# Cross-attention, first batch: the root in two halves, rows scaled on two engines, and new orders around the first scores

## What is computed

```python
Sim = (e @ w1)[:, :, None] + (ctx @ w2)[:, None, :] + einsum('bid,bjd->bij', e * w3, ctx) + b_sim   # e = layernorm(x)
A = softmax(Sim, axis=2)
hq_hat = einsum('bij,bjd->bid', A, ctx)
Batt = softmax(max(Sim, axis=2), axis=1)
hc_bar = einsum('bi,bid->bd', Batt, e)                       # one row for each batch
hcq = concat([e, hq_hat, e * hq_hat, e * hc_bar]) @ W_qv + b_qv
x = x + tanh(g_xattn) * hcq
x = x + tanh(g_ffn) * expert_attention(layernorm(x))         # 8 heads, 5 experts; not touched by the change
```

## Time and profile before

| | |
|---|---|
| time, median of 3 runs | 1182.5 us (1181.83 to 1182.51) |
| the profiled execution's own time | 1181.56 us |
| its span, first to last instruction | 1179.8 us |
| PE busy | 1165.9 us (99%) |
| DVE, ACT, POOL busy | 834.1, 647.7, 657.9 us (71%, 55%, 56%) |
| granted clock of TensorE, mean | 1.000 |

### The profile page before, as it was taken

One profiled execution on the slowest core, in us unless ns is written; L12 is line 12 of the kernel. 1 busy time (PEld: TensorE's weight loads), 2 busy tenths in 40 slices (PEclk: granted clock), 3 DMA queues, 4 the chain that ended last, 5 costly groups with the idle time before them and its releaser, 6 DMA issues.

```text
span 1179.8 us, 19684 instructions
## 1 busy us (share of the span) xinstructions
PE 1165.9 (99%) x6377; PEld 909.4 (77%) x6377; DVE 834.1 (71%) x1518; ACT 647.7 (55%) x1444; POOL 657.9 (56%) x476
## 2 busy tenths in 40 slices
PE   7999999999999999999999999999999999999998
PEld 6888888888888888877767777677677777777765
DVE  7888787878787857465775766666666765765868
ACT  6534343434343434477656566557657666665654
POOL 2625242424242425459298397497497396495594
PEclk9999999999999999999999999999999999999999
DMA  5341413132323224401002002002002011020020
GB/s 201 139 134 53 127 65 113 68 110 70 107 78 99 80 63 157 149 8 37 1 5 103 0 18 89 0 27 80 0 36 71 0 58 49 0 71 0 0 72 36
DMA packets 40749, 75.92 MB, mean 64 GB/s; under 512 B 3728, under 2 KB 4240, under 8 KB 40720
## 3 DMA queue, kind: packets, MB, share of 16 engines
q1 hardware_dynamic: 40720, 75.55, 19.2%
HBM read 58.76 MB, written 16.78 MB: 64 GB/s over the span
## 4 chain that ended last, share of the span: by engine, by line
PE 94%; DVE 4%; issue 1%; ACT 1%; DMA 0%; DVEq 0%; SPq 0%
PE ps_f L945 22%; PE ps_r L2018 13%; PE ps_o L2088 9%; PE ps_s L2075 8%; PE ps_s L2067 8%; PE ps_h L945 7%; PE ps_s L945 7%; PE ps_r L2027 6%; PE ps_r L2051 4%; PE ps_r L2033 1%; PE ps_r L2009 1%; PE ps_r L2041 1%; DVE z_tmp L1705 1%; DVE z L1705 1%; PE ps_t L998 1%
## 5 line engine op out<-in xcount | busy, mean ns | idle before, releaser
L1691 DVE TENSOR_REDUCE nmax<-ps_s 128x1 f32<-128x512 f32 x256 | 158.8, 683 | 112.9 <-PE ps_s L2067 111.9
L1522 ACT ACTIVATE tmp<-ps_s,nmax 128x512 f32<-128x512 f32 x256 | 172.7, 687 | 94.1 <-DVE nmax L1691 94.1
L1465 POOL TENSOR_TENSOR z<-z,z_tmp 128x1280 f32<-128x1280 f32 x35 | 102.9, 2941 | 166.2 <-DVE z_tmp L1705 163.9
L1447 POOL TENSOR_TENSOR spare<-xv,pick 128x512 f32<-128x512 f32 x160 | 169.4, 1059 | 35.6 <-DVE pick L1800 22.7
L1453 POOL TENSOR_TENSOR spare<-spare 128x512 f32<-128x512 f32 x128 | 181.7, 1419 | 10.0
L1531 ACT ACTIVATE pt<-ps_s 128x512 f32<-128x512 f32 x256 | 132.1, 612 | 10.5 <-PE ps_s L2075 10.5
L2075 PE MATMUL ps_s<-ident,tmp 128*128 128x128 f32 x1024 | 122.3, 273 | 0.0
L2075 PEld LDWEIGHTS ps_s<-ident,tmp 128*128 128x128 f32 x1024 | 115.4, 140 | 8.6 <-issue 1.6
L2088 PE MATMUL ps_o<-pt,spare 128*64 128x512 f32 x496 | 113.3, 598 | 0.0
L253 POOL TENSOR_TENSOR e_t<-e_t 128x512 fp32r<-128x512 f32 x28 | 35.4, 1299 | 136.4 <-ACT e_t L493 136.4
L2067 PE MATMUL ps_s<-k,q 64*128 64x512 f32 x768 | 107.0, 409 | 0.1
(11 more groups left out here) (234 smaller groups left out, 2119.4 us busy)
## 6 DMA issues: line engine op xcount, KB each, us to landing
stage<-in_x SPq DMA_DIRECT2D x32, 256.0 KB, 3.1
x_sb<-in_x SPq DMA_DIRECT2D x8, 1024.0 KB, 5.2
x_dram<-x_sb SPq DMA_DIRECT2D x32, 256.0 KB, 2.9
stage<-x_dram SPq DMA_DIRECT2D x8, 1024.0 KB, 5.5
x_sb<-x_dram SPq DMA_DIRECT2D x8, 1024.0 KB, 5.4
out_dram<-x_sb SPq DMA_DIRECT2D x32, 256.0 KB, 2.0
stage<-in_ctx_t SPq DMA_DIRECT2D x28, 256.0 KB, 3.0
stage<-in_ctx SPq DMA_DIRECT2D x28, 256.0 KB, 2.6
```

Of the source, the lines that this page charges most:

```text
L1447: pool.tensor_tensor(v_tmp[:] if e else acc, xv[:, :, e, :].unsqueeze(2).broadcast_to(shape), pick[:, 0, e, :, 2 * p:2 * p + 2].unsqueeze( ...
L1465: pool.tensor_tensor(zv, zv, z_tmp[:, h % 2], ALU.add).then_inc(z_pool, 1)
L1522: act.activation(probs[:, n % BANKS, :], ps_s[:, n % BANKS, :], ACT.Exp, bias=nmax[:, n:n + 1], accum_out=den[:, h, t:t + 1]).then_inc(p_e ...
L1691: dve.tensor_reduce(nmax[:, n:n + 1], ps_s[:, n % BANKS, :], AX_X, ALU.max, negate=True).then_inc(nmax_ready, 1)
```

## The change

It touches the first batch of cross-attention alone; the loop over the other batches keeps its instructions and their order, and only some waits of POOL ahead of it differ. The number of matmuls is the same but for the filling transpositions, of which 45 (18+12+3+3+3+6) become 37 (18+8+4+2+3+2).

- SP loads x tiles 0 and 1, then two blocks of transposed context, then `w_cols`, then the other x tiles and blocks.
- The inverse root is taken for tiles 0 and 1 alone, all 17 steps; for tiles 2 and 3 the steps are strewn between other work of DVE. DVE has 17 more tiny instructions.
- `first_scaled` of tiles 0, 1 and 2 moves to ACT (four ACTIVATE Identity of 128 columns with a scale and a bias column); tile 3 stays on DVE, and its last instruction waits for the tile before.
- PE starts to fill after one tile's statistics and not three; the turning of tiles 2 and 3 moves into the scores of tile 1, ahead of its last three matmuls; `turn_a(1)` and `turn_a(2)` stand together behind `scores(3)`.
- On ACT, casts of context, of weights and of the turned probabilities have new places; `probs_hi` of tiles 1, 2 and 3 stand together at the end.
- On DVE, the root of the second batch runs as a whole behind `row_totals`; `first_row_lo`, `row_weights_max` and the second batch's `normalise_x` have new places in `attended`: tiles 2 and 3 are normalised behind `row_shares`.
- POOL's first `add_bias` waits for `wec_lo` and no longer for `wec_ready`, and the next two for the row dots of the second batch.

```diff
-                elif not first:
+                else:
...
+            def load_first_x(tiles):
+                for t in tiles:
+                    sp.dma_start(stage[:, t, :], of(x_dram, 0)[:, t, :]).then_inc(slot_loaded[t], 16)
+
+            def load_first_ctx_t(tiles):
+                for k in tiles:
...
-            load_x(0, True)
+            load_first_x((0, 1))
+            load_first_ctx_t((0, 1))
             sp.dma_start(w_cols[:], w_sim_cols).then_inc(cols_loaded, 16)
-            load_first_ctx_t()
+            load_first_x((2, 3))
+            load_first_ctx_t((2, 3))
...
-            pool.wait_ge(wec_ready, ND)
+            pool.wait_ge(wec_lo, ND)
             add_bias(0, 0)
+            pool.wait_ge(ew1_ready, 2 * NT)
             add_bias(0, 1)
             add_bias(0, 2)
...
+            def first_scaled(t):
+                act.wait_ge(et_ps, t + 1)
+                if t == 0:
+                    act.wait_ge(cols_loaded, 16)
+                for k in range(ND):
+                    last = act.activation(tmp[:, k, t * P:(t + 1) * P], first_turned[t][:, k, :], ACT.Identity,
+                                          bias=w2_col[:, k:k + 1], scale=w3_col[:, k:k + 1])
+                last.then_inc(es_ready, 1)
...
+            def first_root(half, parts):
+
+                tiles = slice(2 * half, 2 * half + 2)
+                for part in parts:
+                    if part == 0:
+                        dve.wait_ge(stats_done, 2 * half + 2)
+                    mean_rstd(dve, part, stats[:, tiles, :], D, mean[:, tiles], work[:, :, tiles], rstd[:, tiles],
+                              newton if half else first_newton, 0)
+
+            def first_normalise(t):
+                dve.wait_ge(newton if t >= 2 else first_newton, ROOT_STEPS)
...
+                    if k == ND - 1:
+
+                        dve.wait_ge(es_ready, t)
                     last = dve.tensor_scalar(tmp[:, k, t * P:(t + 1) * P], first_turned[t][:, k, :], w3_col[:, k:k + 1],
...
-                normalise_x(0, 0)
-                normalise_x(0, 1)
+                row_stats(0, 0, True)
+                row_stats(0, 1, True)
+                first_root(0, range(ROOT_PARTS))
+                first_normalise(0)
+                first_normalise(1)
+                row_stats(0, 2, True)
+                row_stats(0, 3, True)
                 ctx_t_lo(0, 0, True)
-                first_scaled(0)
+                first_root(1, range(5))
+                first_scaled_lo(0)
                 ctx_t_lo(0, 1, True)
-                normalise_x(0, 2)
-                first_scaled_lo(0)
+                first_root(1, (5, 6))
                 ctx_t_lo(0, 2, True)
+                first_root(1, (7,))
                 ctx_t_lo(0, 3, True)
-                first_scaled(1)
-                normalise_x(0, 3)
+                first_root(1, (8,))
                 first_scaled_lo(1)
+                first_root(1, (9, 10))
                 row_max(0, 0)
-                first_scaled(2)
+                first_root(1, (11, 12, 13))
+                first_normalise(2)
+                first_normalise(3)
                 invert(0, 0)
+                first_scaled(3)
...
+                    if t == 1:
+                        if k == ND - 1:
+
+                            turn_e(0, 2, True)
+                            turn_e(0, 3, True)
+                        return
...
-            pe.wait_ge(stats_done, 3)
+            pe.wait_ge(stats_done, 1)
             fill(18)
             turn_e(0, 0, True)
             turn_e(0, 1, True)
-            fill(12)
+            fill(8)
```

More of the change, by code:

```diff
@@ L280, in _, with load_x @@
         def _(sp):
-            def load_x(b, first=False, second=False):
+            def load_x(b, second=False):
                 for t in range(NT):
@@ L302, in load_ctx @@
                     sp.dma_start(stage[:, t, :], of(c_dram, b)[:, t, :]).then_inc(slot_loaded[t], 16)
-            def load_first_ctx_t():
-                for k in range(ND):
+            def load_first_x(tiles):
[3 more added lines that the diff above has]
+                for k in tiles:
                     sp.dma_start(x_sb[:, k, :], of(ct_dram, 0)[:, k, :]).then_inc(ct0_loaded[k], 16)
@@ L782, in first_softmax @@
                 invert(0, 3)
+                row_stats(1, 3)
+                probs_lo(0, 1)
                 probs_lo(0, 2)
-                row_stats(1, 3)
-                for part in range(5):
-                    root(1, part)
                 probs_lo(0, 3)
@@ L789, in first_softmax @@
                 row_totals(0)
-                for part in range(5, ROOT_PARTS):
+                for part in range(ROOT_PARTS):
                     root(1, part)
-                first_row_lo(1, 1)
-                first_row_lo(2, 2)
             def softmax(b, more):
@@ L851, in attended @@
                     row_shares(b, range(1, ND - 1))
-                for k in range(ND):
-                    if first and k == 1:
-                        row_weights_max(b)
-                    dve.wait_ge(ht_hi, b * ND + k + 1)
-                    dve.tensor_tensor(h_t2[:, 1, k, :], ps_h[:, k % 2, :], h_t2[:, 0, k, :].bitcast(F32),
-                                      ALU.subtract).then_inc(ht_lo, 1)
-                    dve.tensor_tensor(tmp[:, k, :], ps_h[:, k % 2, :], e_t[:, k, :], ALU.mult).then_inc(eh_ready, 1)
-                    if not first and k == 0:
-                        row_shares(b, (ND - 1,))
-                    if more and k < ND - 1:
-                        normalise_x(b + 1, k)
-                if first:
-                    row_shares(b, range(ND))
-                if more:
-                    normalise_x(b + 1, ND - 1)
+                    for k in range(ND):
+                        attended_half(b, k)
+                        if k == 0:
+                            row_shares(b, (ND - 1,))
+                        if more:
+                            normalise_x(b + 1, k)
                 dve.wait_ge(wraw_loaded, 2 * 16)
@@ L897, in keep_stats @@
                                   ALU.mult).then_inc(all_stats_done, 1)
-            for t in range(NT):
-                row_stats(0, t, True)
-            for part in range(ROOT_PARTS):
-                root(0, part)
             first_softmax()
@@ L985, in scores @@
                 product(ps_s[:, t % 2, :], lambda l, k: es_t2[:, l, k, t * P:(t + 1) * P],
-                        lambda r, k: c_t2[:, r, k, :], True, True, ready if t == 0 else None).then_inc(s_ready, 1)
+                        lambda r, k: c_t2[:, r, k, :], True, True, ready if t == 0 or first and t == 1 else None).then_inc(s_ready, 1)
             def turn_a(b, t, first):
@@ L1085, in softmax @@
                     return
[L1086 to L1098 removed]
+                scores(b, 1, True)
+                first_dots(0)
+                fill(4)
+                scores(b, 2, True)
+                turn_a(b, 0, True)
+                scores(b, 3, True)
+                turn_a(b, 1, True)
+                turn_a(b, 2, True)
+                first_dots(1)
+                fill(2)
+                first_dots(2)
+                fill(3)
+                turn_a(b, 3, True)
+                fill(2)
                 first_dots(NT - 1)
[L1101 removed]
+            pe.wait_ge(stats_done, 1)
             fill(18)
```

81 lines of the change are left out of this document (44 added, 37 removed).

## The result

The changed kernel takes 1184.3 us (1183.31 to 1185.05, 22 runs), the kernel before 1182.11 us (1181.43 to 1182.78, 22 runs): 2.2 us or 0.18% slower, ratio 1.0018 with a 95% interval of 1.0012 to 1.0024. That is 0.1 us outside the range given.

The account below looks back on a forecast made before the run. The prediction took PE to bound the kernel: 1.9 us won at the head, less 1.0 and 0.85, left 0.0 or -0.1 at `attend`. From a median of 1182.5 it forecast 1182.3 us, range 1180.9 to 1184.2.

Parts of the forecast that it names:

- The head: First batch ahead of `attend`: scores of tile 0 start at 12.4 instead of 14.19, 1.8 us earlier.
- the lead: Time won at the head: 1.9 us, with 1.0 paid back to ACT's scaling and 0.85 to the place of `probs_hi(1)`.
- rival B: TensorE's clock falls or rises late after PE's 10.2 to 12.4 gap: 1184.2 to 1185.3 us; chance 0.10.
- I cost all this at nothing: New orders of DVE and POOL behind `attend`: no cost; without its cover 0.2 to 0.7 us.
- rival C: New waits behind `attend` and ACT's scaling at its dear end: +0.7 to +1.5 us; chance 0.14.
- the sum: All terms up to the start of `attend`: a change of 0.0, or -0.1 us.
- Rival A: The head's lead lasts: `attend` at 32.9 or earlier, 1180.7 us if all 1.8 us lasted; chance 0.14.

Follow-up runs that it names:

- e2_probs: The changed kernel with `probs_hi` of tile 1 ahead of the exponential of tile 3 and its low half earlier: 1182.9 us (before 1182.20).
- e1_fills: The changed kernel with more filling transpositions behind its last scores (3, 3, 6 and 6): 1183.06 us (before 1182.20).
- e4_before_thin: The kernel before with the changed kernel's few fillings behind the scores of tile 3 (none, 2, 3 and 2): 1182.26 us (before 1182.20).
- e10_fills_behind: e1_fills with everything behind the start of `attend` in the order of the kernel before: 1181.56 us (before 1181.93).
- e8_fills_all: e1_fills with POOL's waits as before the change and tile 2 normalised ahead of the row shares: 1182.71 us (before 1181.96).
- e12: e2_probs with POOL's waits as before, `fill(4)`, and tiles 0, 1 and 2 normalised one place earlier each: 1181.61 us (before 1181.95).
- e11_behind_only: The changed kernel with its few fillings and only the orders behind `attend` undone: 1183.71 us (ratio 1.0015).
- e13: e12 with POOL's first `add_bias` behind `wec_lo` again and the other two right behind it: 1181.89 us (before 1182.06).
- e14: e13 without POOL's wait for the second batch's root: 1187.56 us in 5 runs (before 1182.06).
- e3_both: The changed kernel with the edits of e1_fills and e2_probs together: 1183.03 us (before 1182.20).
- e7: e2_probs with POOL's waits as before, tile 2 normalised ahead of the row shares, and 4 fillings for 2 ahead of the last dots: 1181.93 us (before 1181.96).
- e9: The kernel with e7's fillings and early `probs_hi`, and everything behind `attend` as before the change: 1183.66 us (ratio 1.0015).

## Why the prediction was wrong, step by step

**The head was right.** The turn of tile 0 started at 8.50 for 8.30 (the first statistics at 3.60 and not 3.32: the load, not the root), the scores of tile 0 at 12.44 for 12.4, those of tile 2 at 21.12 for 21.35, the turn of tile 3's probabilities at 31.18 for 31.35, with a wait for the low half of 0.74 us for 0.9. Four scalings on ACT, priced at 1.6 us from rows of other shapes, took 1.51:

```profile
9.20 1.51 ACT L482 ACTIVATE tmp<-ps_t,w_cols 128x128 f32<-128x128 f32 x4 [1.91 <-PE ps_t L1010]
...
11.79 1.49 ACT L482 ACTIVATE tmp<-ps_f,w_cols 128x128 f32<-128x128 f32 x4
...
18.10 1.51 ACT L482 ACTIVATE tmp<-ps_f,w_cols 128x128 f32<-128x128 f32 x4 [0.50 <-PE ps_f L1010]
```

The Trainium skill's formula (ScalarE: Activation LUTs, What ACT_TABLE_LOAD costs), by which I had estimated 1.64 us, comes out 0.13 above that; DVE's 1.37 is the cheaper, as it had implied. `attend` itself came at 33.68, 0.3 us later than the forecast, because the dots ahead of it already ran at the lower clock (the low half that it needs was there at 33.25). And `probs_hi(1)` behind the last division did eat the lead: e2_probs moves it and `attend` starts at 32.32.

**The first step that failed: the change was costed with the clock at 1.00 throughout, and rival B, the fall, was looked for in one place only.** I looked for the fall of the clock in the gap from 10.2 to 12.4, and that was the wrong place. PE stood 1.95 us there and the clock stayed at 1.00. The stretch at 30 to 32 us I never costed as clock: the diff takes 3, 3, 3 and 6 fillings to 0, 2, 3 and 2, and I had written that fillings hide waits, so that fewer of them seemed free. There they keep the clock up. I priced the fall at 1.8 to 2.85 us; the first product of `attend` took 5.03 us for 2.84, 2.2 more, and of that the changed kernel keeps 1.3 in the end: e1_fills, which only adds fillings, is 0.9 us above its kernel before where the change is 2.2 above it, and its clock never falls; the two kinds of execution of e4_before_thin lie 1.9 apart (1183.7 and 1181.8). The Trainium skill (TensorE: Matmul & The Clock Gate, What's actually happening) says that idleness lowers the clock; now a row shows a fall as well (1.00, then 0.50 behind 31.5 us), though not at PE's longest pause since its first work, the 1.95 us.

**The second is the term "I cost all this at nothing" behind `attend`.** Without its cover I had 0.2 to 0.7 us. With the clock held, the new order there costs 0.9 us against the kernel before (e1_fills), inside what rival C, new waits behind `attend`, was priced at (0.7 to 1.5, though part of that was for a dear scaling on ACT), and putting the stretch back as it was is worth 1.2 us (e10_fills_behind 0.4 below). Three of its parts came out otherwise. The normalised tile 3 was to be ready near 51.4, with one tile at 1.21 us beside POOL; both tiles met POOL and took 2.67 us, to 52.07. The `wec` chain was to start 0.8 us later and started 1.4 later; of that the quicker low halves gave 0.9 back (1.48 us for 2.39), foreseen at 1.1. And I had asked only whether the row dots meet `add_bias`: one of four did (1.77 us), as I had it, but what stands behind them, a bias sum and a scaling ahead of the residual, met the other two `add_bias` and lost 2.2 us. The two stops, 0.38 and 0.89 us, add up to 1.27.

Which of the new orders is to blame is shown only in part. Undoing POOL's waits and putting tile 2 ahead of the row shares gained 0.1 us (e8_fills_all, 0.75 above its kernel before); undoing the rest as well, the root in two pieces, `first_row_lo` ahead of `attend`, and a tile normalised behind each product, gained the other 1.1. The traces point to the normalisation of tile 2 inside DVE's unbroken stretch, and e12, where it stands outside, has no stop at the turn of tile 3. The share of the root and of `first_row_lo` was not tested by itself.

In the changed kernel itself only 0.47 us of idle time shows, at the residual. The slow first product gives DVE and POOL time to catch up, so the two losses need not add. Against their own kernels before, the first alone undone gives 1.3 us, the second alone 0.4 (e11_behind_only, +1.8), both 2.6 (e10, -0.4): 0.8 more than their sum, though with intervals of 1 us to either side the medians alone do not show this.

**What the head is worth.** With both losses undone, e10 is 0.4 us below the kernel before, and its interval holds 1. So the change without its side effects is no measurable gain, as the sum had it, with `attend` at 33.82 in e10's trace. Rival A's sign, an `attend` at 32.5 or before, was met by e12 and e13 (32.3 and 32.2), and yet they are at 1181.61 and 1181.89, 0.3 and 0.2 us below the kernel before, within the noise: a microsecond of lead at `attend` is not carried on, because DVE has no idle time left behind it and loses the lead in collisions with a POOL that does not start earlier. That a lead at `attend` is worth its length in the end, which rival A and the whole sum took for granted, was wrong as well.

**What stays open.** Why the clock falls in one execution of a kernel and not in another (5 of 11 in e4_before_thin, 6 of 11 in e2_probs), and at the start of `attend` in e14's trace with PE's rows of e13 up to there. That more fillings ahead of the first product hold it in nearly all executions is shown (0 falls in 11 in e1_fills and e3_both, 1 in 11 in e8_fills_all and e10_fills_behind, 22 in 22 without them); what exactly the chip asks of them is not. Whether some other order carries the lead was not found in three tries (e7, e12, e13). After e12 the one to try would end the second batch's root earlier, so that POOL's chain moves with the lead; e9 was near it, but lost its lead ahead of `attend`.

## What to carry to other kernels

Filling matmuls ahead of the first full-rate product do more than cover a wait. Price their removal by the granted clock behind them, with most of a product's length as the worse case (2.2 us for a product of 2.84 here), and compare the mean clock of every execution, not only of the profiled one.

Find the stretch in which an engine never stands idle. Work that an order moves from a pause into that stretch delays everything behind it by its full length, wherever in the stretch it stands.

When a wait is changed so that one engine starts at another moment, list what the engine that it slows down does at that moment, down to its smallest instructions. And a lead is carried on only if the other engines of the stretch start earlier too.

## What the runs showed of the hardware that I had not expected

- DVE's instructions on 4 columns, 0.15 to 0.23 us with POOL quiet, can take 1.1 to 1.4 us beside a POOL TENSOR_TENSOR (1.12 in e9, 1.36 in e1, 1.21 to 1.26 in e14). In e14 POOL's four from 34.53 to 39.56 take 1.28 us each, and DVE's lengthened instructions end within 0.05 us of the end of one of them (35.83, 37.07, 38.33, 39.58): each seems to stand until POOL's current instruction is over, and in a chain of tiny steps the next one meets the next. Not every one is hit: in the changed kernel the bias sum that reads PSUM took 0.22 us (33.86), with POOL busy from 33.12 to 34.39.
- The granted clock fell from 1.00 to 0.50 in a stretch in which PE had short matmuls with pauses under 1 us, and held through 1.95 us of rest at 10 to 12 us. A rest of about the same length at another place, 1.97 us ahead of `attend` in e9's trace, did have a fall in it (the clock reads 0.65 from 34.0 to 34.5 us and 0.50 behind).
- A stop of PE can cost more than the idle time listed ahead of its next matmul: 0.57 us by starts where the bracket says 0.36.
